# Latent attention with a quantised product on one core: the inverse sums of a head travel by a store and a broadcast load

## What is computed

```python
def layer(x):                                  # x: 4 x 1024 x 128, fp32
    x = x + attention(layernorm(x))
    return x + ffn(layernorm(x))

def attention(x):                              # 16 heads of 8 columns, latent 32
    q, k, v = x @ Wq, x @ Wk, x @ Wv
    latent = (k + v) @ W_down_kv
    k, v = latent @ W_up_k, latent @ W_up_v
    scores = clip(heads(q) @ heads(k).T * scale) * exp(-1e-4 * |i - j|)
    return softmax(clip(scores)) @ heads(v) @ Wo   # softmax over 1024 keys

def ffn(x):                                    # scale, round to fp8, product, scale, bias
    return fp8(x / s_in) @ fp8(W / s_k) * (s_in * s_k) + bias
```

## Time and profile before

| | before |
|---|---|
| median of 3 runs | 519.67 us |
| profiled execution: time | 519.81 us |
| profiled execution: span from first to last instruction | 518.0 us |
| ScalarE busy | 484.7 us (94%) |
| TensorE matmuls busy | 478.4 us (92%) |
| VectorE busy | 270.4 us (52%) |
| GpSimd busy | 218.7 us (42%) |
| mean granted TensorE clock | 0.987 |
| transfers | 73.8 MB, mean 142 GB/s |

### The profile page before, as it was taken

One profiled execution on the slowest core, in us unless ns is written; L12 is line 12 of the kernel. 1 busy time (PEld: TensorE's weight loads), 2 busy tenths in 40 slices (PEclk: granted clock), 3 DMA queues, 4 the chain that ended last, 5 costly groups with the idle time before them and its releaser, 6 DMA issues.

```text
span 518.0 us, 9463 instructions
## 1 busy us (share of the span) xinstructions
PE 478.4 (92%) x3452; PEld 112.4 (22%) x3452; DVE 270.4 (52%) x646; ACT 484.7 (94%) x535; POOL 218.7 (42%) x285
## 2 busy tenths in 40 slices
PE   8899999999999999899999999899999989899961
PEld 3312221132222212132122122123121212121220
DVE  6514553556545554445653654545645564455546
ACT  3789999999999999899999999899999999999951
POOL 0889409883810269692530239883100121002110
PEclk9999999999999999999999999999999999999995
DMA  6679989777444206747853123847835222300000
GB/s 180 196 245 219 328 188 234 285 238 224 126 108 114 76 13 198 234 103 241 257 117 90 46 66 127 246 130 249 251 88 127 66 65 68 88 21 2 1 22 24
DMA packets 57395, 73.79 MB, mean 142 GB/s; under 512 B 6976, under 2 KB 33024, under 8 KB 57344
## 3 DMA queue, kind: packets, MB, share of 16 engines
q1 hardware_dynamic: 56256, 72.72, 49.0%
q10 hardware_dynamic: 1088, 0.41, 0.3%
HBM read 35.40 MB, written 35.65 MB: 137 GB/s over the span
## 4 chain that ended last, share of the span: by engine, by line
PE 39%; ACT 33%; issue 11%; DVE 7%; POOL 4%; SPq 3%; DMA 3%; DVEq 0%; ACTq 0%; POOLq 0%
ACT probs L790 32%; PE ps L990 20%; PE ps L974 12%; DVE ps L1233 2%; PE ps L970 2%; PE ps L887 1%; PE ps L850 1%; PE ps L882 1%; DMA kp_dram<-parts 1%; POOL sq L614 1%; SPq L477 1%; DVE pv_out L1241 1%; POOL sq L626 1%; POOL parts L628 1%; PE ps L854 1%
## 5 line engine op out<-in xcount | busy, mean ns | idle before, releaser
L790 ACT ACTIVATE probs<-ps 128x1024 f32<-128x1024 f32 x512 | 473.6, 1101 | 8.9 <-DVE ps L1233 5.7
L990 PE MATMUL ps<-probs,V 128*9 128x512 f32 x2048 | 267.8, 595 | 1.0 <-ACT probs L790 0.6
L1233 DVE TENSOR_TENSOR ps<-ps,consts 128x256 f32<-128x256 f32 (+1 forms) x256 | 140.6, 563 | 160.9 <-PE ps L974 154.4
L974 PE MATMUL ps<-Qs,Ks 64*128 64x512 bf16 x992 | 172.2, 384 | 16.8 <-ACT probs L790 14.6
L974 PEld LDWEIGHTS ps<-Qs,Ks 64*128 64x128 bf16 x992 | 44.5, 93 | 286.9 <-ACT probs L790 275.2
L1241 DVE COPY pv_out<-ps 105x512 f32<-105x512 f32 x31 | 21.4, 691 | 60.0 <-PE ps L990 59.9
L592 POOL TENSOR_SCALAR rs<-mv 128x4 f32<-128x4 f32 (+1 forms) x10 | 2.3, 229 | 99.9 <-DVEq L1415 99.3
L990 PEld LDWEIGHTS ps<-probs,V 128*9 128x9 f32 x2048 | 30.5, 88 | 63.4 <-issue 53.9
L675 POOL TENSOR_TENSOR xs<-xs,magic 128x512 f32<-128x512 f32 x7 | 8.9, 1276 | 58.5 <-DVE magic L1294 58.5
L688 POOL TENSOR_TENSOR yb<-yb,bias_s 128x512 bf16<-128x512 bf16 x7 | 8.1, 1156 | 49.9 <-DVE yb L1366 49.5
L628 POOL TENSOR_TENSOR parts<-sq,parts 128x1024 bf16<-128x1024 f32 (+1 forms) x16 | 28.3, 1771 | 1.3
(11 more groups left out here) (148 smaller groups left out, 280.5 us busy)
## 6 DMA issues: line engine op xcount, KB each, us to landing
Qs<-qp_dram SPq DMA_DIRECT2D x58, 256.0 KB, 4.9
qp_dram<-parts SPq DMA_DIRECT2D x14, 768.0 KB, 6.1
Ks<-kp_dram SPq DMA_DIRECT2D x28, 256.0 KB, 3.9
kp_dram<-parts SPq DMA_DIRECT2D x12, 384.0 KB, 4.2
kp_dram<-parts SPq DMA_DIRECT2D x6, 768.0 KB, 5.0
Ks<-kp_dram SPq DMA_DIRECT2D x34, 128.0 KB, 2.9
qp_dram<-parts SPq DMA_DIRECT2D x7, 512.0 KB, 8.0
X<-L_attn_x SPq DMA_DIRECT2D x9, 256.0 KB, 2.9
```

The source lines that it names most:

```text
L790: nc.scalar.activation(probs[:, quad % RING, 2 * jp:2 * jp + 2, :].rearrange("p j n -> p (j n)"), ps_all[:, bank * CH:(bank + 2) * CH], AC ...
L974: last = nc.tensor.matmul(bank, Ks[half, g, jp, key_cols(v, kc)], Qs[half, g, jp, qh, v, :], start=True, stop=True)
L990: last = nc.tensor.matmul(pv[32 * j:32 * j + VW, :], V[:, unit // 2 * NB + kc, HG * j + g, :], probs[:, quad % RING, j, :], start=i == 0, ...
L1233: nc.vector.tensor_tensor(own, own, factors, ALU.mult).then_inc(fixed, 1)
```

## The change

The inverses no longer go through TensorE. SyncE stores `rec` (128 rows of 64) to a buffer in memory, waits until it has landed, and loads it back so that each of the 8 rows of a head gets all 512 inverses of that head. VectorE's second step (`widen_sums`), TensorE's job "sp" and the two constants that they need are gone; VectorE multiplies `o_raw` by the loaded tile instead of the bank, in the same quad 11. SyncE's new steps stand at the head of a unit, before the gather of its first group.

```diff
 for _u in range(1, UNITS):
     JOBS += [(_u * UNIT_QUADS + _q, _k, _u - 1) for _q, _k in (
-        (10, "sp"), (14, "proj"), (TAIL_ROWS[_u], "xqT"), (TAIL_PRODUCTS[_u], "y"))]
+        (14, "proj"), (TAIL_ROWS[_u], "xqT"), (TAIL_PRODUCTS[_u], "y"))]
...
-        consts = sb("consts", [P, 4 * P + 32 + P + HD])
+        consts = sb("consts", [P, 4 * P + 32])
...
+            def spread_inverse_sums(unit):
+
+                sp.wait_ge(rec_ready, unit + 1)
+                sp.dma_start(rec_dram[unit], rec[:, :]).then_inc(rec_out, 16)
+                sp.wait_ge(rec_out, 16 * (unit + 1))
+                if unit > 0:
+                    sp.wait_ge(ot_ready, unit)
+                sp.dma_start(wide[:, :], rec_dram[unit].rearrange("(h c) t -> h (c t)", c=HD)
+                             .rearrange("h (o n) -> h o n", o=1).broadcast_to([H, HD, CH])).then_inc(spread, 16)
...
                     group = unit * G + g
+                    if unit > 0 and g == 0:
+                        spread_inverse_sums(unit - 1)
                     if unit < UNITS - 1:
                         gather(group)
...
-            def spread_sums(unit, bank):
-                pe.wait_ge(spread, unit + 1)
-                nc.tensor.matmul(bank, same_head, wide[:, :], start=True, stop=True).then_inc(spread_ps, 1)
-
...
-                step(nc.vector.reciprocal(rec[:, :], den[:, unit % 2, :]))
-
-            def widen_sums(unit):
-                settle()
                 if unit > 0:
-                    dve.wait_ge(spread_ps, unit)
-                nc.vector.tensor_tensor(wide[:, :].rearrange("p (c t) -> p c t", c=HD),
-                                        rec[:, :].rearrange("p (o t) -> p o t", o=1).broadcast_to([P, HD, CH // HD]),
-                                        place.rearrange("p (c o) -> p c o", o=1).broadcast_to([P, HD, CH // HD]),
-                                        ALU.mult).then_inc(spread, 1)
+                    dve.wait_ge(rec_out, 16 * unit)
+                nc.vector.reciprocal(rec[:, :], den[:, unit % 2, :]).then_inc(rec_ready, 1)
 
             def divide_by_sums(unit):
-                dve.wait_ge(spread_ps, unit + 1)
-                nc.vector.tensor_tensor(OT[:, unit % 2, :], o_raw[:, unit % 2, :], work, ALU.mult).then_inc(ot_ready, 1)
+                dve.wait_ge(spread, 16 * (unit + 1))
+                nc.vector.tensor_tensor(OT[:, unit % 2, :], o_raw[:, unit % 2, :], wide[:, :], ALU.mult).then_inc(ot_ready, 1)
...
                 if at == 7:
                     invert_sums(unit)
-                    widen_sums(unit)
+                elif at == 11:
+                    divide_by_sums(unit)
```

More of the change, by code:

```diff
@@ L147, in build @@
 def build(nc, x, wq, wkT, wvT, wo, wd, wuk, wuv, w8, s_in, s_k, bias, decay_rows, decay_table,
-          const_cols, out, qt_dram, kt_dram, qp_dram, kp_dram):
+          const_cols, out, qt_dram, kt_dram, qp_dram, kp_dram, rec_dram):
     with ExitStack() as ctx:
@@ L187, in build @@
         rows_of = [eye_rows[:, P + g:P + g + 1] for g in range(G)]
-        consts = sb("consts", [P, 4 * P + 32 + P + HD])
+        consts = sb("consts", [P, 4 * P + 32])
         fix_plus, fix_minus = consts[:, 0:2 * P], consts[:, 2 * P:4 * P]
         hsum = consts[:, 4 * P:4 * P + 32]
-        same_head = consts[:, 4 * P + 32:5 * P + 32]
-        place = consts[:, 5 * P + 32:5 * P + 32 + HD]
         eye16 = sb("eye16", [P, P], BF16)
@@ L287, in build @@
         moved = [sem(f"moved{i}") for i in range(2)]
+        rec_ready = sem("rec_ready")
+        rec_out = sem("rec_out")
         spread = sem("spread")
-        spread_ps = sem("spread_ps")
         ot_ready = sem("ot_ready")
@@ L349, in emptied @@
                 return {"T": xnT_ready, "q": q_sb, "k": k_sb, "v": v_sb}[kind], i + 1
-            if kind in ("sp", "proj", "xqT", "y"):
-                return {"sp": ot_ready, "proj": x1_ready, "xqT": xqT_ready, "y": y_ready}[kind], i + 1
+            if kind in ("proj", "xqT", "y"):
+                return {"proj": x1_ready, "xqT": xqT_ready, "y": y_ready}[kind], i + 1
             return {"turn": turned, "n": tops_ready, "flags": oks_ready, "flag": flag_ready}[kind], i + 1
@@ L383, in _ @@
             sp.wait_ge(fold_in, 48)
-            sp.dma_start(consts[:, :], const_cols[:, P + G:6 * P + 32 + HD + G]).then_inc(const_in, 16)
+            sp.dma_start(consts[:, :], const_cols[:, P + G:5 * P + 32 + G]).then_inc(const_in, 16)
             spread_decay(1, decay_in)
@@ L930, in job @@
                     sum_oks(work)
-                elif kind == "sp":
-                    spread_sums(i, work)
                 elif kind == "turn":
@@ L1353, in empty_work @@
                                             ALU.is_lt).then_inc(flag_ready, 1)
-                elif kind == "sp":
-                    divide_by_sums(i)
                 elif kind == "turn":
@@ L1573, in constants @@
     head_sum = (p // HD == np.arange(32)[None, :]).astype(np.float64)
-    same_head = (p // HD == np.arange(P)[None, :] // HD).astype(np.float64)
-    place = (p % HD == np.arange(HD)[None, :]).astype(np.float64)
     rows_of = (p % 32 // HD == np.arange(G)[None, :]).astype(np.float64)
     return {"decay_rows": rows, "decay_table": table,
-            "const_cols": np.concatenate([np.eye(P), rows_of, fix_plus, fix_minus, head_sum, same_head, place], 1)}
+            "const_cols": np.concatenate([np.eye(P), rows_of, fix_plus, fix_minus, head_sum], 1)}
 def kernel(**inputs):
@@ L1602 @@
     kp_dram = nc.dram_tensor("kp_dram", (B, P, PRODUCTS, KN), BF16, kind="Internal").ap()
-    build(nc, *args, out, qt_dram, kt_dram, qp_dram, kp_dram)
+    rec_dram = nc.dram_tensor("rec_dram", (UNITS, P, CH // HD), F32, kind="Internal").ap()
+    build(nc, *args, out, qt_dram, kt_dram, qp_dram, kp_dram, rec_dram)
     r = run_bass_kernel_spmd(nc, [arrays], core_ids=[0])
```

## The result

The changed kernel takes 561.39 us, the median of 4 runs (560.60 to 562.49), against 519.70 us before (519.64 to 519.77): the ratio is 1.080, 95% interval 1.078 to 1.082. That is 41.7 us slower; the forecast was 33.9 slower (553.6, range 541 to 564).

A forecast was written before the change was run, and what follows sets the result against it. ScalarE's stream of exponentials was taken as the bound. Waits of 29.4 us plus 4.5 for TensorE's clock, savings set at zero, gave 33.9 us on the profiled 519.81; forecast 553.6 us against the median, range 541 to 564.

The forecast's parts named there:

- What bounds the kernel: Whole stream: ScalarE's 512 exponentials, 473.6 us, are the bound; an edit matters where it makes ScalarE wait or spares a wait.
- the two kinds of saving: TensorE's removed product, 0.32 us in units 2, 4, 6 and 7; VectorE's removed `widen_sums`, 0.7 in units 3 and 5.
- The savings are lost in the wait: Savings come ahead of the new wait, whose end SyncE sets, so both were set at zero.
- The wait, and SyncE's lateness: Ahead of quad 12's fix in all seven units: VectorE waits for the load, delayed by SyncE's queue; 29.4 us in sum.
- The trip, taken at 5.2 us: Store of inverses 2.4 us, broadcast load 2.7, wake-ups 0.1, once SyncE gets to it; ends 4.1 and 7.6.
- Unit 1, taken at 7.7: Delay of quad 12's fix in unit 1: the inverses' store queues behind three large stores, the third landing at 105.4; 7.7 us.
- Unit 3, 8.9: Delay of quad 12's fix in unit 3: SyncE, with many stores and loads to issue, is free at 224.27; 8.9 us.
- Unit 5, 7.7: Delay of quad 12's fix in unit 5: SyncE is free at 342.94; 7.7 us.
- TensorE's clock: Behind the three long pauses the clock falls, 1.5 us (one quad) each, 4.5 in all; short pauses leave it full.
- The hidden trip: Rival: SyncE takes up inverses at once, the trip ends before the multiply, only 2.7 us of savings remain: 517; chance 0.04.
- the clock that stays down for a unit: Rival: after each long pause TensorE stays at 1.2 GHz for most of a unit: 591, partly so 565 to 591; chance 0.07.
- Queues behind the new waits: SyncE's first gather of the unit is pushed back some 3 us, at no cost; GpSimd and staged loads gain time.

The follow-up runs named there:

- e1_bare: Kernel before without the inverse sums' spread (TensorE's product and `widen_sums` left out), VectorE multiplying by a tile of ones: 516.58 us.
- e2_unwaited: Changed kernel with both transfers made, but the load into a spare tile; VectorE multiplies by ones without waiting for it: 516.82 us.
- e3_trip_first: Changed kernel with SyncE making the round trip ahead of the result's store and the next input's load: 543.65 us.
- e4_store_twice: Changed kernel with the store of the inverses made and awaited twice, one after the other: 576.57 us.
- e9_scalar_queue_13: Changed kernel with the round trip issued by ScalarE instead of SyncE, and VectorE's multiply at quad 13 instead of 11: 526.67 us.
- e7_first_and_late: Changed kernel with the trip ahead of the result's store and next input's load, multiply at quad 14, projection at 15: 524.60 us.

## Why the prediction was right, point by point

**What bounds the kernel.** Right. ScalarE's 474 us did not move, and the two kinds of saving are as read: 0.7 us from the product's share in e1_bare, where 4 x 0.32 = 1.3 was forecast in the rival's sum, and 2.6 from `widen_sums`, where 1.4 was.

**The savings are lost in the wait.** Right where it can be seen. The pauses ahead of quad 8 did shrink by 2.6 us, and those ahead of quad 12 in units 3 and 5 grew by as much, since their end hangs on SyncE.

**The wait, and SyncE's lateness.** Right in kind in all seven units, and shown by e2_unwaited (no wait, no loss), e3_trip_first (other order, four pauses gone) and e4_store_twice. In size the sum was 34.3 instead of 29.4 us:
- The trip, taken at 5.2 us, took 5.7 to 6.2 in units 2 to 7 (in unit 3 5.9: store 2.7, load 3.2 by its issues), on a median store of 2.6 and load of 3.2 us. It was short by 0.5 to 1.0 us in each of the six. In units 4, 6 and 7 little of it is to be seen (1.48, 1.29 and 1.11 against 1.3, 1.3 and 1.2), and that is partly luck: unit 4's own rows before would have given 1.0 and not 1.3, and the result's store landed in 4.8 and 4.3 us in units 6 and 7, where it took 5.2 and 5.0 before. The fit in the Trainium skill, "DMA: Bandwidth & Descriptors", section on the anatomy of one DMA, gives an estimate of 4.7 us for the two transfers; the page states it for transfers that GpSimd issues, and the ones that SyncE issues here take longer in both parts.
- Unit 1, taken at 7.7, was 5.91: the store behind the three large ones landed at 103.24, 4.67 us after its issue, and not at 105.4. That a later transfer lands only after an earlier one's full 7.7 us was too much.
- Unit 3, 8.9 against 12.09: 0.7 from the trip, 0.9 from a result store that took 6.6 us to land instead of 5.8, 0.7 from the slow multiply (below), and 1.3 because the pause ahead of quad 8 was no longer there, less some 0.4, by which SyncE came to that store sooner against the stream than before. Unit 5, 7.7 against 10.27, has the same trip and saving, and 0.5 from the multiply.

**TensorE's clock.** The term was the most mis-sized: 4.5 us forecast, 8.6 measured. What failed is "three times 1.5", one quad at the low level: the level lasted some 8 us after ScalarE went on (in unit 3 from 244.94 to the end of the stretch from 250, which has 0.53), and each long pause cost 2.3 to 2.5 us. And it fell in unit 2 too, behind a pause of 2.14 us, which the text had excluded; that cost 1.3. The Trainium skill, "TensorE: Matmul & The Clock Gate", section on what's actually happening, has the gate at half rate by default and released by activity; the rows at 236 and 240 agree, with no matmul in either and a clock of 0.90, then 0.50.

**How the misses add up.** The forecast was 7.8 us too low: 4.9 in the long pauses and 4.1 in the clock, less the 2.6 ahead of quad 8, which were set at zero. Of the other 1.4 us, 0.8 is what the profiled execution (560.6) lies below the median; the rest is not traced. The two large terms missed in the same direction, so the time is near the upper end of the range.

**The rivals.** The hidden trip needed SyncE to be free 1.3 us sooner in unit 2, and e3_trip_first, which makes it so, loses nothing in that unit. Nothing of the clock that stays down for a unit was seen; it came back within 10 us each time.

**Queues behind the new waits.** Right: the late first gather cost nothing (e2_unwaited).

## What to carry to other kernels

A round trip through memory took 5.7 to 6.2 us here for a store of 32 KB and a load of 256 KB (8.0 behind three large stores; other sizes weren't tried). What decides more than its length is when the queue that issues it gets to it: read that queue's timeline at the place, with every store and landing wait ahead of it. An engine that is idle half of the time is no place for a wait if the engine that bounds the kernel has only one or two steps in hand; move the wait behind slack first, and count what the move puts beside the critical steps (here 0.44 us a unit, as much as the removal is worth, or 1.57, three times as much). A pause of the bounding engine also starves TensorE, and its clock then costs a few us more, which work that nobody reads can prevent.

## What was not expected of the hardware

**A multiply that took up to 3.4 times as long.** VectorE's multiply took 0.68 us in all 7 units before, with one operand in PSUM. In the changed kernel, with both in SBUF, it took 0.69 to 1.41 us, and 2.33 us in e9_scalar_queue_13. GpSimd's timeline in unit 3 of the changed kernel:

```profile
239.95 1.89 POOL L681 TENSOR_TENSOR sq<-qT 128x1024 f32<-128x1024 f32 x1 [0.18 <-POOL parts L639]
241.80 1.89 POOL L682 TENSOR_TENSOR sq<-kT 128x1024 f32<-128x1024 f32 x1
```

The second product of GpSimd ends at 243.69, and VectorE's multiply, begun at 242.83, ends at 244.24, as long after it as it takes alone less 0.1 us. The Trainium skill, "SBUF — State Buffer", section "Who interferes with whom", says that a VectorE instruction with two inputs in SBUF contends with a GpSimd one that reads SBUF, and that the second to come waits for the first to end. The times agree with this. In unit 5, and three times in e9_scalar_queue_13, the multiply began while GpSimd was in an instruction, and ended 0.54 to 0.56 us after it. In unit 1 of that run GpSimd's ran from 104.75 to 107.09, and the multiply from 105.31 to 107.64. In units 2, 4, 6 and 7 of the changed kernel GpSimd had no work at that time, and the multiply took 0.69. That is a comparison of units, not a run in which only GpSimd's work was taken away.

**A short pause can bring the clock down, and need not.** In the changed kernel the clock was 0.56 behind the pause of 2.14 us in unit 2, and full behind those of 1.48, 1.29 and 1.11 us.

```profile
171.00:174.00 3.00, 1.06 (x12) 0.19 (x4) 1.38 (x3) 2.13 (x3) 0.00 (x0) 1.00 0.10 17
174.00:177.00 3.00, 3.00 (x16) 1.91 (x18) 0.70 (x2) 2.56 (x3) 0.00 (x0) 0.56 0.61 159
```

TensorE did 1.06 us of work in the 3 us ahead of it. Length alone does not decide: in e7_first_and_late the clock stayed full behind a pause of 2.41 us, in which TensorE had the projection to do (1.61 us of work from 229 to 232).
